# A tile's token numbers go through a second buffer that Pool empties behind its wait for landed additions

## The chip, the cores and the metric

The kernel runs on one core of a Trainium2 chip. The metric is the device time in microseconds (us) from launch to end. The engines are named as in the profile: PE (TensorE, matmuls), DVE (VectorE), ACT (ScalarE), POOL (GpSimd) and SP (SyncE, which here only issues transfers).

## The reference

Four attention layers and a feed-forward layer run over 8 sequences of 256 tokens with 256 features. The last layer is a mixture of 8 experts, each token going to its best two:

```python
def _moe(x, rw, rb, w1, b1, w2, b2):
    xf = x.reshape(T, D)
    router_weights = jax.nn.softmax(xf @ rw + rb, axis=-1)
    topw, topi = jax.lax.top_k(router_weights, K)              # K = 2 of E = 8
    topw = jax.nn.softmax(topw, axis=-1)
    combine = jnp.zeros((T, E), xf.dtype).at[jnp.arange(T)[:, None], topi].add(topw)
    h = jax.nn.gelu(jnp.einsum('td,edf->etf', xf, w1) + b1[:, None, :], approximate=False)
    eo = jnp.einsum('etf,efd->etd', h, w2) + b2[:, None, :]
    out = jnp.einsum('etd,te->td', eo, combine)
...
x = _layernorm(x + _moe(x, router_w, router_b, e_w1, e_b1, e_w2, e_b2), ln3_g, ln3_b)
```

## The kernel before, in words

The first part (attention, feed-forward, router) ends by writing every token's row twice into `slots_x` in DRAM, sorted by expert and cut into tiles of 256 rows. Beside its 256 features a row carries three more words: its token number, its expert and its share. The second part, `moe_part`, works off 23 such tiles, numbered n = 0 to 22, and then normalises the sum in `x_rows` and stores it.

For each tile, `moe_part` reads the expert's weights `w1` and `w2` (1 MB each) from DRAM, splits each weight and each activation in a high and a low half (ACT rounds, `first_high`, `second_high`, `rows_high`; DVE subtracts, `first_low`, `second_low`, `rows_low`, `hidden_low`) and multiplies on PE with three matmuls for each product. The work is laid out as a pipeline: while PE does `up` of tile n, it does `down` of tile n - 1. Each engine has its own instruction order, written out by hand, in a loop over pairs of tiles (`i` is the tile's parity and picks one of two buffers), and semaphores alone tie the engines together. The orders within one step n are:

- PE: `up(n)`, `turn(n + 1)` (transposes), `down(n - 1)`.
- ACT: four quarters, each `first_high(n + 1)`, then GELU and its high half for tile n; `rows_high(n + 1)`; `second_high(n)`.
- DVE: four times `first_low(n + 1)` and `hidden_low(n)`; `rows_low(n + 1)`; `second_low(n)`; then `row_data(n)`; then `add_bias(n - 1)`.
- POOL: `add_rows(n - 1)`.
- SP, each fetch for tile n + 2 behind a wait: rows, `w1`, then (once `second_low(n)` is done) `w2`, then (once `row_data(n)` is done) the three words of the rows (`about`), then `b1`, then (once `add_bias(n - 1)` is done) a bias; then three register loads that pick the next expert, and the next step.

`row_data` (L1416 to L1426) copies the token numbers to `token[i]`, which Pool's indirect transfers read, and works out `share[i]`. `add_bias` (L1433) moves PE's result from PSUM to `result[i]`. `add_rows` (L1237 to L1247) multiplies `result[i]` by `share[i]` (L1241), drains, waits until the additions of the tile before have landed, and issues two indirect transfers (L1247) that add 128 rows each to `x_rows`. Their semaphore is `added[i]`; an addition counts once it has landed. As two tiles can hold the same token, the additions of one tile start only when those of the tile before are in.

Of the kernel before, what the change touches and what calls it, by code (L numbers as in the profile page):

```python
# [10 lines left out]
U32 = mybir.dt.uint32  # L11
# [5 lines left out]
P = 128  # L17
# [14 lines left out]
GT = GROUP // P  # L32
# [114 lines left out]
def build(nc, t, out):  # L147
    with ExitStack() as ctx:
        def sb(name, shape, dt=F32):
            return ctx.enter_context(nc.sbuf_tensor(name, shape, dt))  # L150

        x_rows = nc.dram_tensor("x_rows", [P * ALL_TILES + 2 * GROUP, D], F32).ap()
        slots_x = nc.dram_tensor("slots_x", [X_TILES * GROUP, ROW], F32).ap()
        ident = sb("ident", [P, P])
        minus_half = sb("minus_half", [P, TILES])
        eps = sb("eps", [P, TILES])
        w1, w2 = sb("w1", [P, KC, FF]), sb("w2", [P, FC, D])
        b1_expert = sb("b1_expert", [P, E, FC + 1])
        tile_expert = sb("tile_expert", [P, PLACES], I32)
        tile_source = sb("tile_source", [P, PLACES], I32)  # L160
        shared = (ident, minus_half, eps, w1, w2, b1_expert, tile_expert, tile_source)
        attention_part(nc, t, x_rows, slots_x, *shared)
        moe_part(nc, t, out, x_rows, slots_x, *shared)
# [915 lines left out]
def moe_part(nc, t, out, x_rows, slots_x, ident, minus_half, eps, w1_first, w2_first, b1, tile_expert, tile_source):  # L1079
    with ExitStack() as ctx:  # L1080
        def sb(name, shape, dt=F32):
            return ctx.enter_context(nc.sbuf_tensor(name, shape, dt))

        def two(name, shape, dt=F32):
            return [sb(f"{name}{i}", shape, dt) for i in range(2)]

        def sem(name):
            return ctx.enter_context(nc.semaphore(name))
# [10 lines left out]
        about = two("about", [P, GT, ROW - D])  # L1099
# [1 line left out]
        hidden = sb("e_hidden", [P, FC, GROUP])  # L1101
        hidden_hi, hidden_lo = two("e_hidden_hi", [P, FC, GROUP], F32R), two("e_hidden_lo", [P, FC, GROUP], F32R)
        result = two("result", [P, GT, D])
        token = two("token", [P, GT], U32)
        chosen = two("e_chosen", [P, GT])
        share = two("share", [P, GT])

# [9 lines left out]
        gate = sem("gate")  # L1117
# [17 lines left out]
        b1_loaded = [sem(f"b1_loaded{i}") for i in range(2)]  # L1135
        down_full = sem("down_full")
        row_data_ready = sem("row_data_ready")
        result_ready = sem("result_ready")
        added = [sem(f"added{i}") for i in range(2)]
        z_loaded = [sem(f"z_loaded{b}") for b in range(B)]  # L1140
# [6 lines left out]
        ADDED = 16 * GT  # L1147
# [87 lines left out]
        @block.gpsimd  # L1235
        def _(pool):
            def add_rows(n, i, nth):  # L1237

                pool.wait_ge(result_ready, n + 1)
                pool.sem_inc(gate, 1)  # L1240
                pool.tensor_tensor(result[i][:], result[i][:], share[i][:].unsqueeze(2).to_broadcast([P, GT, D]), ALU.mult)  # L1241
                pool.drain()  # L1242

                pool.wait_ge(added[1 - i], ADDED * nth)
                pool.sem_inc(gate, 1)
                for m in range(GT):
                    pool.indirect_dma_start(x_rows, bass.IndirectOffsetOnAxis(ap=token[i][:, m:m + 1], axis=0), result[i][:, m, :], None, compute_op=ALU.add).then_inc(added[i], 16)  # L1247

            for i in range(2):
                pool.memset(result[i][:], 0.0)  # L1250
                pool.iota(token[i][:], pattern=[[1, GT]], base=P * ALL_TILES + i * GROUP, channel_multiplier=GT)
            pool.drain()
            pool.sem_inc(gate, 1)
            for i in range(2):
                for m in range(GT):
                    pool.indirect_dma_start(x_rows, bass.IndirectOffsetOnAxis(ap=token[i][:, m:m + 1], axis=0), result[i][:, m, :], None).then_inc(added[i], 16)
            with pool.Fori(0, PAIRS) as j:
                for i in (1, 0):
                    n = j * 2 + 2 - i

                    add_rows(n - 1, 1 - i, j + 2 - i)
            add_rows(last_tile, 0, PAIRS + 1)

            def inverse_root(pair):
                both = slice(pair * 2 * TILES, (pair + 1) * 2 * TILES)
                pool.wait_ge(var_ready, pair + 1)
                pool.tensor_tensor(rstd[:, both], var_eps[:, both], minus_half[:, 0:1].to_broadcast([P, 2 * TILES]), ALU.pow).then_inc(rstd_ready, 1)  # L1267

            def gain_of(b):
                pool.wait_ge(normal_ready, b + 1)  # L1270
                pool.tensor_tensor(z[b][:], z[b][:], gain[:].unsqueeze(1).to_broadcast([P, TILES, D]), ALU.mult).then_inc(gained, 1)  # L1271

            pool.wait_ge(norm_loaded, 16 * 2)
            inverse_root(0)
            inverse_root(1)
            gain_of(0)
            inverse_root(2)
            gain_of(1)
            gain_of(2)
            inverse_root(3)  # L1280
            for b in range(3, B):
                if b not in GAIN_BY_DVE:
                    gain_of(b)
# [114 lines left out]
        def _(dve):  # L1398
            def first_low(s, i, q):
                dve.wait_ge(w1_hi_ready, s * QUARTERS + q + 1)  # L1400
                cols = slice(q * 2 * P, (q + 1) * 2 * P)
                dve.tensor_tensor(w1_lo[i][:, :, cols], w1[i][:, :, cols], w1_hi[i][:, :, cols].bitcast(F32), ALU.subtract).then_inc(w1_lo_ready, 1)

            def second_low(s, i, q):
                dve.wait_ge(w2_hi_ready, s * QUARTERS + q + 1)
                dve.tensor_tensor(w2_lo[i][:, 2 * q:2 * q + 2, :], w2[i][:, 2 * q:2 * q + 2, :], w2_hi[i][:, 2 * q:2 * q + 2, :].bitcast(F32), ALU.subtract).then_inc(w2_lo_ready, 1)  # L1406

            def rows_low(n, i):
                dve.wait_ge(rows_hi_ready, n + 1)
                dve.tensor_tensor(rows_lo[i][:].rearrange("p k g -> p (k g)"), turn_bank[i][:], rows_hi[i][:].bitcast(F32).rearrange("p k g -> p (k g)"), ALU.subtract).then_inc(rows_lo_ready, 1)  # L1410

            def hidden_low(n, i, q):
                dve.wait_ge(hidden_hi_ready, n * QUARTERS + q + 1)
                dve.tensor_tensor(hidden_lo[i][:, 2 * q:2 * q + 2, :], hidden[:, 2 * q:2 * q + 2, :], hidden_hi[i][:, 2 * q:2 * q + 2, :].bitcast(F32), ALU.subtract).then_inc(hidden_lo_ready, 1)  # L1414

            def row_data(i, nth, loads):  # L1416

                dve.wait_ge(about_loaded[i], 16 * loads)
                dve.wait_ge(b1_loaded[i], 16 * loads)
                dve.wait_ge(added[i], ADDED * nth)  # L1420
                dve.tensor_copy(token[i][:], about[i][:, :, 0].bitcast(U32))  # L1421
                dve.tensor_scalar(chosen[i][:], about[i][:, :, 1], b1_e[i][:, FC:FC + 1], 1.0, ALU.is_equal, ALU.subtract)
                dve.drain()  # L1423
                dve.tensor_tensor(chosen[i][:], chosen[i][:], about[i][:, :, 2], ALU.add)  # L1424
                dve.drain()
                dve.scalar_tensor_tensor(out=share[i][:], in0=chosen[i][:], scalar=-1.0, in1=chosen[i][:], op0=ALU.mult, op1=ALU.max).then_inc(row_data_ready, 1)  # L1426

            def add_bias(n, i, nth):

                dve.wait_ge(b2_loaded[i], 16 * nth)  # L1430

                dve.wait_ge(down_full, n + 1)
                dve.tensor_tensor(result[i][:], down_bank[i][:].rearrange("p (g d) -> p g d", g=GT), b2_e[i][:].unsqueeze(1).to_broadcast([P, GT, D]), ALU.add).then_inc(result_ready, 1)  # L1433

# [7 lines left out]
                    rows_low(1, 1)  # L1442
            for q in range(QUARTERS):
                second_low(0, 0, q)
            row_data(0, 1, 1)
            with dve.Fori(0, PAIRS) as j:
                for i in (1, 0):
                    n = j * 2 + 2 - i
                    for q in range(QUARTERS):
                        first_low(n + 1, 1 - i, q)  # L1450
                        hidden_low(n, i, q)
                    rows_low(n + 1, 1 - i)
                    for q in range(QUARTERS):
                        second_low(n, i, q)
                    row_data(i, j + 2 - i, j + 2 - i)
                    add_bias(n - 1, 1 - i, j + 1)
            add_bias(last_tile, 0, PAIRS + 1)

            def moments(b):
# [98 lines left out]
```

## Time and profile before

| | |
|---|---|
| median of 3 runs | 1256.54 us (1251.69 to 1257.38) |
| profiled execution: its time, its span | 1253.78 us, 1252.0 us |
| mean granted TensorE clock | 0.950 of full speed |
| busy share of the span: PE, DVE, ACT, POOL | 88%, 66%, 58%, 40% |
| attention part | 0 to 910 us of the span |
| expert tiles, first addition of biases to the last but one | 941.06 to 1207.50 us |
| last additions landed, final norm begins | 1224.58 us |

Time is counted from the start of the span. A step is one round of the expert loop, one tile; 21 steps lie between the two add-bias operations of the table's sixth row, so one takes 12.69 us on average. The busy shares are means over parts with different limits, so only the stretch from 910 us on speaks about the change.

### The profile page before, as it was taken

The page shows a single profiled execution, that of the slowest core. Times are in us where ns is not written, and L with a number is a line of the kernel's source. Part 1 is how long each engine was busy: PE and PEld are TensorE (multiplying, and loading weights), DVE is VectorE, ACT ScalarE, POOL GpSimd, SP SyncE. Part 2 cuts the span into 40 slices and gives each one's busy share as a digit, 9 for nine tenths or more (in the row PEclk, how much of TensorE's full clock was granted, in tenths as well). Part 3 has the DMA queues.
Part 4 walks back from the last instruction along what each step waited for, and adds up shares of the span by engine and source line. Part 5 has one row for each costly group of instructions (what it writes and reads, how often), then busy time and mean ns, then how long its engine had stood idle before and what let it go on. Part 6 is the DMA issues. An engine that isn't in the chain of part 4 may idle for free. (4 is left out here: it accounts for less than half of the span.)

```text
span 1252.0 us, 27029 instructions
## 1 busy us (share of the span) xinstructions
PE 1105.5 (88%) x8981; PEld 910.5 (73%) x8981; DVE 823.3 (66%) x2495; ACT 729.1 (58%) x1537; POOL 501.6 (40%) x709
## 2 busy tenths in 40 slices
PE   8688889999999999998889988977969999999960
PEld 7466667767888878876667756655869899999960
DVE  2667878775555555557776777752457788887846
ACT  4345555665555554545566755645177787887842
POOL 4344555332111223335565455323313334343444
PEclk9789999999999999999999999977889999999985
DMA  7575747564234333435756556504367687867764
GB/s 165 87 117 129 118 71 104 77 127 60 47 45 56 52 52 52 86 53 81 143 88 93 86 88 101 86 27 162 133 231 212 181 232 208 240 206 221 219 189 143
DMA packets 110313, 152.35 MB, mean 122 GB/s; under 512 B 23041, under 2 KB 94977, under 8 KB 103425
## 3 DMA queue, kind: packets, MB, share of 16 engines
q1 hardware_dynamic: 101712, 140.21, 51.2%
q0 software_dynamic: 8352, 10.80, 4.5%
q8 instruction: 56, 0.92, 0.3%
q14 instruction: 49, 0.39, 0.2%
q10 hardware_dynamic: 144, 0.02, 0.0%
HBM read 78.39 MB, written 21.62 MB: 80 GB/s over the span
## 5 line engine op out<-in xcount | busy, mean ns | idle before, releaser
L875 ACT ACTIVATE probs<-s 128x384 f32<-128x384 f32 (+1 forms) x512 | 265.9, 542 | 194.2 <-PE s L683 173.6
L946 DVE TENSOR_REDUCE neg_max<-s 128x2 f32<-128x512 f32 x256 | 169.7, 689 | 94.5 <-PE s L658 84.9
L683 PE MATMUL s<-q_stack,k_stack 98*128 98x256 bf16 (+1 forms) x1024 | 177.6, 263 | 14.4 <-ACT probs L875 13.3
L541 POOL TENSOR_SCALAR_AFFINE_SELECT probs<-probs 128x256 f32<-128x256 f32 x256 | 102.3, 409 | 180.3 <-ACT probs L875 180.3
L943 DVE CUSTOM_DVE_ANT_0 s<-s,mask_qk 128x256 f32<-128x256 f32 x256 | 114.2, 446 | 87.0 <-PE s L655 79.5
L1299 PE MATMUL moe<-rows_hi,e_w_hi 128*128 128x256 f32 x368 | 106.6, 290 | 17.2 <-DVE rows_lo L1410 17.2
L683 PEld LDWEIGHTS s<-q_stack,k_stack 98*128 98x128 bf16 x1024 | 91.3, 99 | 40.2 <-ACT probs L875 24.4
L702 PE MATMUL pv<-probs,v 128*32 128x256 f32 (+1 forms) x2048 | 116.5, 370 | 4.0 <-POOL probs L541 3.9
L658 PE MATMUL s<-k_stack,q_stack 96*128 96x256 bf16 x512 | 98.0, 276 | 13.0 <-DVE neg_max L946 11.3
L1299 PE MATMUL moe<-e_w_hi,e_hidden_hi 128*128 128x256 f32 x368 | 104.7, 284 | 1.2 <-DVE e_w_lo L1406 1.2
L604 PE MATMUL work<-hT,w_qk 128*128 128x256 f32 x384 | 96.1, 395 | 10.2 <-ACTq L797 10.2
L1299 PE MATMUL moe<-rows_lo,e_w_hi 128*128 128x256 f32 x368 | 105.1, 286 | 0.0
L1299 PE MATMUL moe<-rows_hi,e_w_lo 128*128 128x256 f32 x368 | 104.9, 285 | 0.0
L1299 PE MATMUL moe<-e_w_lo,e_hidden_hi 128*128 128x256 f32 x368 | 102.9, 280 | 0.0
L1299 PE MATMUL moe<-e_w_hi,e_hidden_lo 128*128 128x256 f32 x368 | 102.7, 279 | 0.0
L1247 POOL DMA_INDIRECT x_rows<-result,token x46 | 84.1, 1828 | 35.4 <-issue 31.5
L702 PEld LDWEIGHTS pv<-probs,v 128*32 128x32 f32 x2048 | 62.4, 113 | 46.0 <-issue 21.9
L1414 DVE TENSOR_TENSOR e_hidden_lo<-e_hidden,e_hidden_hi 128x512 fp32r<-128x512 f32 x92 | 81.0, 880 | 20.6 <-ACT e_hidden_hi L1374 17.1
L1241 POOL TENSOR_TENSOR result<-result,share 128x512 f32<-128x512 f32 x23 | 30.3, 1316 | 155.9 <-DVE result L1433 155.9
L654 PE MATMUL s<-k_stack,q_stack 96*128 96x256 bf16 x256 | 71.5, 281 | 22.4 <-DVE neg_max L944 17.3
L604 PEld LDWEIGHTS work<-hT,w_qk 128*128 128x128 f32 x384 | 71.7, 196 | 22.7 <-ACTq L797 12.2
L1299 PEld LDWEIGHTS moe<-rows_hi,e_w_hi 128*128 128x128 f32 x368 | 72.3, 197 | 20.0 <-issue 18.1
(194 smaller groups left out, 2696.9 us busy)
## 6 DMA issues: line engine op xcount, KB each, us to landing
w<-in_expert_w SPq DMA_DIRECT2D x26, 1024.0 KB, 5.4
k_stack<-k_part SPq DMA_DIRECT2D x192, 128.0 KB, 4.1
q_stack<-q_part SPq DMA_DIRECT2D x192, 128.0 KB
e_w<-in_expert_w SPq DMA_DIRECT2D x24, 1024.0 KB
rows<-slots_x SPq DMA_DIRECT2D x25, 256.0 KB
slots_x<-filler SPq DMA_DIRECT2D x8, 518.0 KB
cT<-in_context SPq DMA_DIRECT2D x16, 256.0 KB, 4.5
e_b<-in_expert_b SPq DMA_DIRECT2D x24, 128.0 KB
```

Source lines behind the costliest of these rows:

```text
L541: pool.affine_select(out=blocks, in_=blocks, compare_op=ALU.is_ge, fill=0.0, base=0, pattern=[[0, TILES], [1, P]], channel_multiplier=-1). ...
L604: last = pe.matmul(dst[:, half * S:(half + 1) * S], w[:, k, half * P:(half + 1) * P], src[:, k, :], start=(k == 0), stop=(k == KC - 1))
L654: pe.matmul(dst[:, 0:S], q[:, P:S], k, start=True, stop=True)
L658: last = pe.matmul(dst[:, qt * S:(qt + 1) * S], q[:, qt * P:(qt + 1) * P], k, start=True, stop=True)
L683: last = pe.matmul(dst[:, kt * S:kt * S + S - q0], k[:, kt * P:(kt + 1) * P], q[:, q0:S], start=True, stop=True)
L702: last = pe.matmul(pv[32 * j:32 * j + 32, g * S + q0:(g + 1) * S], v[n % 3][:, kt, hd, :], probs[hd][:, kt * S:kt * S + S - q0], start=(kt ...
L875: act.activation(probs[hd][:, 0:width], s2[hd % 2][:, 0:width], ACT.Exp, scale=SCALE).then_inc(probs_ready, 1)
L943: dve.tensor_tensor_reduce(src[:, 0:S], src[:, 0:S], mask_qk[:].rearrange("p b s -> p (b s)"), -1.0, -MASKED, ALU.add, ALU.min, neg_max[:, ...
L946: dve.tensor_reduce(neg_max[:, :, hd], src[:].rearrange("p (t s) -> p t s", t=TILES), AX_X, ALU.max, negate=True).then_inc(s1_free, 1)
L1247: pool.indirect_dma_start(x_rows, bass.IndirectOffsetOnAxis(ap=token[i][:, m:m + 1], axis=0), result[i][:, m, :], None, compute_op=ALU.add ...
L1299: last = pe.matmul(dst, lhs[a], rhs[b], start=first and m == 0, stop=end and m == 2)
L1414: dve.tensor_tensor(hidden_lo[i][:, 2 * q:2 * q + 2, :], hidden[:, 2 * q:2 * q + 2, :], hidden_hi[i][:, 2 * q:2 * q + 2, :].bitcast(F32), ...
```

## The change

DVE now writes the token numbers to a new buffer `token_next[i]`, and Pool copies them to `token[i]` behind its wait for the landed additions of the tile before. A new semaphore, `row_data_taken`, tells DVE that `token_next[i]` (and with it `share[i]`) has been used. The wait for `added[i]` leaves `row_data`, and `add_bias` gets one, on the buffer that it is about to overwrite, which is that of tile n - 3 in step n.

```diff
-        token = two("token", [P, GT], U32)
+        token, token_next = two("token", [P, GT], U32), two("token_next", [P, GT], U32)
...
             def add_rows(n, i, nth):
 
+                pool.wait_ge(row_data_ready, n + 1)
                 pool.wait_ge(result_ready, n + 1)
                 pool.sem_inc(gate, 1)
                 pool.tensor_tensor(result[i][:], result[i][:], share[i][:].unsqueeze(2).to_broadcast([P, GT, D]), ALU.mult)
...
                 pool.wait_ge(added[1 - i], ADDED * nth)
                 pool.sem_inc(gate, 1)
+                pool.tensor_copy(token[i][:], token_next[i][:]).then_inc(row_data_taken, 1)
+                pool.drain()
                 for m in range(GT):
...
             pool.drain()
-            pool.sem_inc(gate, 1)
+            pool.sem_inc(row_data_taken, 1)
...
                 dve.wait_ge(b1_loaded[i], 16 * loads)
+                if nth is not None:
+                    dve.wait_ge(row_data_taken, nth)
+                dve.tensor_copy(token_next[i][:], about[i][:, :, 0].bitcast(U32))
...
             def add_bias(n, i, nth):
 
                 dve.wait_ge(b2_loaded[i], 16 * nth)
                 dve.wait_ge(added[i], ADDED * nth)
-                dve.tensor_copy(token[i][:], about[i][:, :, 0].bitcast(U32))
...
-            row_data(0, 1, 1)
+            row_data(0, None, 1)
...
-                    row_data(i, j + 2 - i, j + 2 - i)
+                    row_data(i, n, j + 2 - i)
                     add_bias(n - 1, 1 - i, j + 1)
```

On DVE, at the end of the loop's first step (odd n, so tile n is in buffers 1), the rows before the change are these; `added1` counts the landed additions of tile n - 2:

```order
L1406 TENSOR_TENSOR e_w2_lo1<-e_w2,e_w2_hi1 128x512 [waits w2_hi_ready] x4
L1418 ISA
L1420 REGISTER_ALU [waits b1_loaded1,about_loaded1]
L1421 COPY token1<-about1 128x2 [waits added1]
L1422 TENSOR_SCALAR e_chosen1<-about1,e_b1_1 128x2
L1424 TENSOR_TENSOR e_chosen1<-e_chosen1,about1 128x2
L1426 SCALAR_TENSOR_TENSOR share1<-e_chosen1 128x2
L1433 TENSOR_TENSOR result0<-moe4,e_b2_0 128x512 [waits down_full,b2_loaded0]
```

And these with the change, where `added0` counts the landed additions of tile n - 3:

```order
L1410 TENSOR_TENSOR e_w2_lo1<-e_w2,e_w2_hi1 128x512 [waits w2_hi_ready] x4
L1422 ISA
L1426 COPY token_next1<-about1 128x2 [waits row_data_taken,b1_loaded1,about_loaded1]
L1427 TENSOR_SCALAR e_chosen1<-about1,e_b1_1 128x2
L1429 TENSOR_TENSOR e_chosen1<-e_chosen1,about1 128x2
L1431 SCALAR_TENSOR_TENSOR share1<-e_chosen1 128x2
L1436 REGISTER_ALU [waits b2_loaded0]
L1438 TENSOR_TENSOR result0<-moe4,e_b2_0 128x512 [waits down_full,added0]
```

The instructions keep their places; the wait for additions has moved from the copy to the last row, and to an older tile.

On Pool, in the loop's second step and the last tile, the rows before are these:

```order
L1241 TENSOR_TENSOR result1<-result1,share1 128x512
L1244 ISA
L1247 DMA x_rows<-result1,token1 2560x256 x2
L1257 REGISTER_ALU
L1257 COMPARE_AND_BRANCH
L1241 TENSOR_TENSOR result0<-result0,share0 128x512
L1247 DMA x_rows<-result0,token0 2560x256 x2
```

And these with the change:

```order
L1243 TENSOR_TENSOR result1<-result1,share1 128x512
L1246 ISA
L1248 COPY token1<-token_next1 128x2
L1251 DMA x_rows<-result1,token1 2560x256 x2
L1261 REGISTER_ALU
L1261 COMPARE_AND_BRANCH
L1243 TENSOR_TENSOR result0<-result0,share0 128x512
L1248 COPY token0<-token_next0 128x2
L1251 DMA x_rows<-result0,token0 2560x256 x2
```

A small copy (and, not printed, a drain) now stands between the wait for the earlier additions and the two transfers. The order on PE, ACT and SP is what it was.

## Rows read from the trace of the kernel before

**Rows 1.** Stretches of the span: PE, PEld, DVE, ACT, POOL busy, clock, DMA

```profile
941.06:1207.50 266.44, 252.29 (x2115) 250.06 (x2115) 211.55 (x379) 213.96 (x441) 105.34 (x63) 0.98 0.75 218
1207.50:1224.58 17.08, 2.35 (x20) 2.15 (x19) 1.39 (x3) 0.00 (x0) 8.41 (x6) 0.64 0.48 106
```

**Rows 2.** Waits from 900 to 1210 us: total us, times, longest us

```profile
DVE token L1421 <- DMA x_rows<-result,token: 37.6, 21, 5.2
ACT e_w_hi L1347 <- DMA e_w<-in_expert_w: 28.2, 11, 5.0
...
ACT e_w_hi L1347 <- DMA w<-in_expert_w: 15.7, 10, 3.0
...
PE moe L1299 <- DVE rows_lo L1410: 17.2, 12, 3.7
```

**Rows 3.** Chain of work that ended last, one step: start us, us, what

```profile
1095.37 0.70 DVE result L1433
1096.22 1.35 POOLq L1242
...
1101.06 5.55 DMA x_rows<-result,token
1107.35 0.70 DVE result L1433
```

**Rows 4.** DVE's timeline, the end of that step and after

```profile
1102.67 0.68 DVE L1410 TENSOR_TENSOR rows_lo<-moe,rows_hi 128x512 fp32r<-128x512 f32 x1
1103.27 2.49 DVE L1406 TENSOR_TENSOR e_w_lo<-w,e_w_hi 128x512 fp32r<-128x512 f32 x4
1106.63 0.17 DVE L1421 COPY token<-about 128x2 uint32<-128x2 uint32 x1 [0.87 <-DMA x_rows<-result,token]
...
1108.56 1.53 DVE L1414 TENSOR_TENSOR e_hidden_lo<-e_hidden,e_hidden_hi 128x512 fp32r<-128x512 f32 x1
```

**Rows 5.** SP's timeline: fetches of w1 (L1162) and w2 (L1165)

```profile
985.58 0.33 SPq L1162 DMA_DIRECT2D e_w<-in_expert_w  x1
...
1088.07 0.33 SPq L1162 DMA_DIRECT2D e_w<-in_expert_w  x1
...
1105.93 0.33 SPq L1165 DMA_DIRECT2D w<-in_expert_w  x1
...
1112.37 0.33 SPq L1162 DMA_DIRECT2D e_w<-in_expert_w  x1
```

**Rows 6.** ACT's timeline: the first rounding of each fetched w1

```profile
994.14 0.63 ACT L1347 ACTIVATE e_w_hi<-e_w 128x512 fp32r<-128x512 f32 x1 [4.99 <-DMA e_w<-in_expert_w]
...
1094.07 0.63 ACT L1347 ACTIVATE e_w_hi<-e_w 128x512 fp32r<-128x512 f32 x1 [2.55 <-DMA e_w<-in_expert_w]
...
1119.41 0.64 ACT L1347 ACTIVATE e_w_hi<-e_w 128x512 fp32r<-128x512 f32 x1 [3.35 <-DMA e_w<-in_expert_w]
```

**Rows 7.** Pool's groups over the whole span: busy, mean ns of one

```profile
L1247 POOL DMA_INDIRECT x_rows<-result,token x46 | 84.1, 1828 | 35.4 <-issue 31.5 <-DMA x_rows<-result,token 3.9
...
L480 POOL TENSOR_TENSOR var_eps_main<-mean_var_main,eps 128x2 f32<-128x2 f32 x24 | 4.7, 197 | 59.9 <-DVEq L905 59.3
...
L1251 POOL IOTA token<- 128x2 uint32 x2 | 0.3, 131 | 0.0
```

**Rows 8.** Tile `token`: transfers' us from issue to landing

```profile
DMA to landing us min/median/max: 3.8/6.4/10.0
```

**Rows 9.** Chain of work that ended last, the tail

```profile
1207.50 0.70 DVE result L1433
...
1218.18 0.74 issue
...
1220.79 3.77 DMA x_rows<-result,token
```

**Rows 10.** Pool's timeline around the change's new copy

```profile
1108.23 1.31 POOL L1241 TENSOR_TENSOR result<-result,share 128x512 f32<-128x512 f32 x1 [5.39 <-DVE result L1433]
1110.64 2.09 POOL L1247 DMA_INDIRECT x_rows<-result,token  x1 [1.10 <-issue]
```

**Rows 11.** A stretch of 2 us behind an idle PE: busy, clock

```profile
1130.00:1132.00 2.00, 2.00 (x14) 2.00 (x13) 1.09 (x2) 0.00 (x0) 0.00 (x0) 0.59 0.77 126
```

More of the change, by code:

```diff
@@ L1137, in moe_part @@
         row_data_ready = sem("row_data_ready")
+        row_data_taken = sem("row_data_taken")
         result_ready = sem("result_ready")
@@ L1419, in row_data @@
                 dve.wait_ge(b1_loaded[i], 16 * loads)
-                dve.wait_ge(added[i], ADDED * nth)
-                dve.tensor_copy(token[i][:], about[i][:, :, 0].bitcast(U32))
+                if nth is not None:
+                    dve.wait_ge(row_data_taken, nth)
+                dve.tensor_copy(token_next[i][:], about[i][:, :, 0].bitcast(U32))
                 dve.tensor_scalar(chosen[i][:], about[i][:, :, 1], b1_e[i][:, FC:FC + 1], 1.0, ALU.is_equal, ALU.subtract)
@@ L1430, in add_bias @@
                 dve.wait_ge(b2_loaded[i], 16 * nth)
+                dve.wait_ge(added[i], ADDED * nth)
                 dve.wait_ge(down_full, n + 1)
```

## The prediction

> **What bounds the kernel now.** I began with the page's split of the span: the change touches only the expert part, so I cut the rest off with the view by stretches. From the first add-bias to the last but one (L1433 at 941.06 and 1207.50 us), 21 steps take 266.44 us, 12.69 us each, and PE is busy for 252.29 of them [rows 1]. So PE leaves 14.2 us, and everything the change can win lies near that figure.
>
> Then the view of waits. DVE stands still 37.6 us, 21 times, before its copy of the token numbers, for additions to land: 1.79 us a step. ACT stands still 28.2 + 15.7 = 43.9 us, 21 times, for `w1`. PE stands still 17.2 us, 12 times, for `rows_lo` of DVE [rows 2].
>
> The chain of waits shows how the first closes on itself: add-bias at 1095.37, Pool's product, the second transfer at 1101.06, its landing after 5.55, and the next add-bias at 1107.35, 11.98 us later [rows 3]. In the 21 steps the last link is always a landing. Yet a chain names only the last releaser; I need to know what is late next.
>
> DVE's and SP's timelines give that. `second_low` ends at 1103.27 + 2.49 = 1105.76, SP issues `w2` at 1105.93, DVE idles 0.87 until the landing, and SP reaches the next `w1` only at 1112.37, since that stands on SP's queue behind `row_data`, behind `add_bias` and behind three register loads [rows 4, 5]. That `w1` is what ACT starts on at 1119.41, and ACT's start at 1094.07 is what led to it [rows 6]. This is a second loop, over two steps: ACT start 1094.07, fetch 1112.37 (18.30 later, 0.87 of it the stall), landing 7.04 later: 25.34 us. The first loop and this one share the stall.
>
> **The change part by part.**
>
> 1. It removes the wait at the token copy: 1.79 us a step [rows 2]. Queued behind it on DVE were the share, add-bias and the next step's `first_low`; waiting on those were Pool (idle anyway until add-bias), SP (`about`, a bias, and behind them `w1`) and ACT through `w1`.
>
> 2. It adds a wait at add-bias for tile n - 3. The landing of tile n - 2 now comes about when DVE gets there, so that of n - 3 came one step, some 12 us, earlier: cost 0. It also adds a wait in `row_data` for Pool's copy for tile n - 2. Pool makes that within 2.4 us of the product's start (its transfer begins at 1110.64 where the product begins at 1108.23 [rows 10]), most of a step ahead of need: cost 0. That cover is gone only if a landing is a whole step late; the longest one took 10.0 against a median of 6.4 [rows 8], 3.6 late. Pool's new wait for `row_data_ready` is always met, since DVE does it before add-bias.
>
> 3. It adds a copy of 128x2 words and a drain on Pool, behind the wait for landing and ahead of the transfers. The trace has no such copy. The nearest rows are the two-input operation of the same size, 0.197 us, and the iota of that size, 0.131 us [rows 7]. For the drain, the gap from the product's end to the transfer is 1.10 us with a drain in it [rows 10], and from a landing to the transfer 0.74 without one [rows 9]: 0.36 at most as a difference, 0 at least. Copy and drain together: 0.13 to 0.56, taken as 0.45, as I see nothing that hides the drain. In a step this is covered: from landing to landing the additions need 0.74 + 1.83 + 0.30 (between the transfers) + 6.4 = 9.3 us [rows 7 to 9], 9.7 with the copy, against 12. Only at the end is it bare: tiles 21 and 22 follow each other without cover, from 1207.50 to the last landing at 1224.56 [rows 9]. Cost 2 x 0.45 = +0.9 us, once.
>
> 4. A price on DVE. While Pool's product ran (1108.23 for 1.31), a `hidden_low` took 1.53 us where others take 0.68, 0.85 more [rows 4, 10]. The new copy lands among the same DVE operations, so it can hold one for up to its own 0.2 us. It would count half in the two-step loop: at most 0.1 x 21 = 2.1 us. I take 0, because DVE idles before several of these for ACT; 2.1 goes into the range.
>
> The Trainium skill speaks against the change here: "SBUF — State Buffer", section "SBUF: two separate sides", says that VectorE with two SBUF inputs and a GpSimd operation that reads SBUF exclude each other for a whole instruction. The 1.53 us row agrees. By that rule each copy costs at some point up to a DVE operation's 0.68 us of waiting on Pool, and the sum would be 0.7 a tile worse in the tail, 1.4 in all, and otherwise the same.
>
> 5. What is late next. The fetch loop without the stall: 2 x 12.69 - 1.79 = 23.6 us, 11.8 a step. Against it, the fetch itself may get slower. From SP's issue to ACT's start took 6.25 us on average over 20 fetches, 5.35 at least and 8.56 at most (985.58 to 994.14; others here are 1088.07 to 1094.07 and 1112.37 to 1119.41 [rows 5, 6]). I sorted these by DVE's stall just before. After the eight stalls up to 1.1 us the fetch took 6.59; after the twelve longer ones 6.03. The stall spaces out `w2` (issued ahead of it) from the additions and `w1` (issued behind it); without it they overlap more. So I add 0.5 us to a fetch, near the difference of 0.56: 24.1 for two steps, 12.04 for one. PE itself needs 252.29 / 21 = 12.01, with stretches at 0.59 of the clock, that is partly at 1.2 GHz, behind its idle times [rows 1, 11]; its steps at full clock took 11.7. PE is thus just under the fetch loop.
>
> **Sum.** 21 x (12.69 - 12.04) = 13.7 us won, 0.9 lost in the tail: 12.8. The profiled execution took 1253.8 us, so 1241.0. The three runs have their median at 1256.5 and reach from 1251.7 to 1257.4; I set the kernel before at 1255, between the two, and forecast **1242**.
>
> **The rivals.**
>
> - *PE is next, not the fetch* (17%). The fetch keeps to 6.0 or less, and with PE never idle its clock holds: 11.7 a step. 21 x 0.99 = 20.8, less 0.9: 19.9, so 1235. For it: fetches of 5.4 us are frequent. Against it: the sorted fetches.
>
> - *The stall moves to the fetch* (18%). With `w2`, additions and `w1` on the queues at once, a fetch gets slower by 1.2 to 1.8 us, most or all of the stall that left the two-step loop, and the step stays at 12.4 to 12.7: 1250 to 1256. For it: two of the fetches took over 7.4 us, one 8.56, all beside additions, and DMA is 75% busy already [rows 1]. Against it: transfers now only move by 1.8 us in a step of 12. That a wait survives under another name (the new semaphore, or add-bias on an old tile) would give the same time; item 2 speaks against it.
>
> - *Slower: the additions become the loop* (8%). They are one behind the other by Pool's wait, and now each has a copy and drain within. It decides once a landing takes over 12.69 - 3.3 = 9.4 us on average; then Pool falls behind, add-bias waits for the older landing and everything with it. At 9.9 the step is 13.2, 21 x 0.5 + 0.9 = 11 us more: 1266. One landing of 10.0 shows that it happens, the median of 6.4 [rows 8] that it isn't the rule.
>
> - The forecast: 57%, from 1238 to 1250 by itself (fetch slower by 0.2 to 1.1 us, copy holding DVE or not).
>
> **How the numbers follow.** A measurement of this kernel can tell about 0.5%, 6.3 us, from no change, so "same" is 1250 to 1263. Faster: the forecast, the PE rival and part of the second, 0.57 + 0.17 + 0.02, less some for spread, 0.75. Same 0.17, slower 0.08. The range for 8 in 10 takes in the PE rival's 1235 and most of the second rival's: 1234 to 1255.
>
> **What would show it.** In the changed kernel DVE's copy to `token_next` has no wait for additions (none of the 37.6 us); PE's wait for `rows_lo` falls from 17.2 us to some 5 and its stretches at the low clock mostly go; ACT still waits for `w1`, some 1.2 us a step instead of 2.1; SP's fetch to ACT's start takes 6.5 to 6.9 on average; the step is 12.0 us; Pool's copy takes 0.13 to 0.2; the tail from the last but one add-bias to the last landing is 18 us rather than 17. I am wrong if fetches take over 8 us (second rival), if Pool waits for landings ahead of its copy in most steps (third), or if a wait for `row_data_taken` or `added` shows on DVE.

## The result and the profile after

The changed kernel took 1232.73 us (median of 4 runs, 1230.59 to 1234.83) against 1254.12 (4 runs, 1247.55 to 1257.38): a ratio of 0.9836, with a 95% interval of 0.9805 to 0.9867, so 1.6% faster. I had forecast 1242 and given 1234 to 1255. In a later batch of runs the same kernel took 1233.06 us, but the kernel before took 1244.35 there: 0.9909, 0.9888 to 0.9930. The new time stayed and the old one moved; what is known of that stands at the end of the account of the prediction.

The view by stretches, cut at the same events as [rows 1] (the first row is added, the time before the first add-bias):

```profile
908.76:940.82 32.06, 24.67 (x169) 24.10 (x170) 20.71 (x40) 25.21 (x49) 5.53 (x8) 0.79 0.66 222
940.82:1186.06 245.24, 245.24 (x2105) 245.24 (x2104) 209.27 (x378) 215.15 (x440) 117.00 (x84) 1.00 0.79 237
1186.06:1204.30 18.24, 3.96 (x34) 3.75 (x32) 1.39 (x3) 0.00 (x0) 8.79 (x8) 0.71 0.49 108
```

The 21 steps fell from 266.44 to 245.24 us, 11.68 each, and PE is busy for all of it at the full clock. PE's busy time itself fell from 252.29 to 245.24. So of the 21.2 us, 14.2 were idle time and 7.0 were busy time, which went as the granted clock rose from 0.98 to 1.00. The tail, from the last but one add-bias to the last landing, grew from 17.08 to 18.24. The first add-bias came 0.24 us earlier than before, and the stretch behind the tail differs by 0.1.

The waits from 900 to 1190 us, the ones that answer to [rows 2]:

```profile
ACT e_hidden L1375 <- PE moe L1303: 11.5, 17, 1.2
...
ACT e_w_hi L1351 <- DMA e_w<-in_expert_w: 8.5, 10, 1.9
...
ACT e_w_hi L1351 <- DMA w<-in_expert_w: 3.7, 4, 1.5
...
PE moe L1303 <- DVE rows_lo L1414: 2.3, 1, 2.3
```

DVE no longer waits for a landing at all, nor for `row_data_taken`. ACT waits 12.2 us for `w1` instead of 43.9, and now waits for PE. PE waits for `rows_lo` once, before the first add-bias. The chain of waits, where [rows 3] had landings, is now PE alone, step after step:

```profile
1108.39 0.44 PE moe L1297 x4
1108.82 11.31 PE moe L1303 x96
1120.13 0.44 PE moe L1297 x4
1120.57 11.11 PE moe L1303 x96
```

Pool's timeline, in a step and in the tail; it answers to [rows 10]:

```profile
1105.35 1.32 POOL L1243 TENSOR_TENSOR result<-result,share 128x512 f32<-128x512 f32 x1 [4.50 <-issue]
1107.15 0.71 POOL L1248 COPY token<-token_next 128x2 uint32<-128x2 uint32 x1 [0.48 <-issue]
1108.66 1.81 POOL L1251 DMA_INDIRECT x_rows<-result,token  x1 [0.80 <-issue]
...
1188.44 0.19 POOL L1248 COPY token<-token_next 128x2 uint32<-128x2 uint32 x1 [0.47 <-issue]
```

The copy takes 0.71 us in a step and 0.19 in the tail, where DVE stands still. From the product's end to the first transfer took 1.10 us before and now takes 1108.66 - 1106.67 = 1.99.

### The profile page after: what moved, and what is told of

Same layout as the page of the kernel before. It is cut to its first block and busy times, and to the rows that moved or that the text cites. A ratio compares the mean times of both kernels' runs of the same rounds, so it can differ in the third digit from the quotient of the medians.

```text
span 1231.6 us, 27064 instructions
## 1 busy us (share of the span) xinstructions
PE 1099.5 (89%) x8981; PEld 907.1 (74%) x8981; DVE 821.4 (67%) x2495; ACT 729.9 (59%) x1537; POOL 513.8 (42%) x732
## 5 line engine op out<-in xcount | busy, mean ns | idle before, releaser
L604 PE MATMUL work<-hT,w_qk 128*128 128x256 f32 x384 | 94.9, 391 | 10.8 <-ACTq L797 10.8
L1418 DVE TENSOR_TENSOR e_hidden_lo<-e_hidden,e_hidden_hi 128x512 fp32r<-128x512 f32 x92 | 76.6, 833 | 39.5 <-ACT e_hidden_hi L1378 30.5
L1251 POOL DMA_INDIRECT x_rows<-result,token x46 | 80.5, 1750 | 25.2 <-issue 25.2
L944 DVE CUSTOM_DVE_ANT_0 s<-s,mask_qk 128x128 f32<-128x128 f32 x256 | 84.9, 332 | 0.0
L1375 ACT ACTIVATE e_hidden<-moe,e_b 128x256 f32<-128x256 f32 x184 | 75.9, 463 | 11.6 <-PE moe L1303 11.5
```

Source lines behind the costliest of these rows:

```text
L604: last = pe.matmul(dst[:, half * S:(half + 1) * S], w[:, k, half * P:(half + 1) * P], src[:, k, :], start=(k == 0), stop=(k == KC - 1))
L944: dve.tensor_tensor_reduce(src[:, S:S + P], src[:, S:S + P], mask_qk[:, 1, :], -1.0, -MASKED, ALU.add, ALU.min, neg_max[:, 0, hd:hd + 1]). ...
```

## The experiments

Each batch has its own runs of the kernel before; ratios are against those. "Step" is the time from the first add-bias to the last but one in the profile, divided by 21.

**The wait put back (e1_wait_back).**

```diff
                     dve.wait_ge(row_data_taken, nth)
+                    dve.wait_ge(added[i], ADDED * loads)
```

> The changed kernel with DVE's wait for the landed additions of tile n - 2 put back in front of the copy in row_data; the second buffer, Pool's copy and its drain stay. Theory: the whole gain is that wait. From the product's end to the first transfer Pool took 1.12 us before and takes 1.99 with the copy and drain, and here these 0.87 us lie in the landing loop again: the step is 12.69 + 0.87 = 13.5 us, and the time is about 18 us above before, near 1272. Rival: something else in the change wins (the later write of token, the wait at add-bias): the time stays near 1233. Second rival: the landing loop has slack besides its stall, and the time is that of before, 1254.

1247.1 us against 1245.05, ratio 1.0022 (1.0003 to 1.0041). The gain is gone, so the wait is what the change wins by. But of the 18 us more only 2 came. That is the second rival's time, yet not for its reason, slack in the landing loop: the profile has DVE's wait for a landing again, in all 21 steps:

```profile
DVE token_next L1427 <- DMA x_rows<-result,token: 40.2, 21, 3.9
```

So the landings must have made up for the 0.87 us by which Pool starts its additions later. From the second transfer's issue to DVE's copy they took 5.32 us on average over the 21 steps (5.31, from 1007.78 to 1013.09, and 4.78, from 1020.13 to 1024.91, in two steps in a row), against 6.42 in the profile of the kernel before. The step is (1198.93 - 939.23) / 21 = 12.37 us. Neither figure compares cleanly with that profile: it is from another batch, in which the kernel before took 9 us more, and it was not profiled beside this run. So how much of the shorter landing is due to the copy's delay stays open.

**Add-bias ahead of row_data, nothing else (e2_swap).**

```diff
-                    row_data(i, j + 2 - i, j + 2 - i)
                     add_bias(n - 1, 1 - i, j + 1)
+                    row_data(i, j + 2 - i, j + 2 - i)
```

> The kernel before with one edit: in DVE's loop add_bias(n - 1) stands ahead of row_data(n), with its wait; no second buffer and no copy. Theory: what costs is that the landing of tile n - 2 holds up add-bias of tile n - 1, and so the next additions. With the order turned, a landing 11.3 us after its add-bias meets a wait 11.68 + 0.7 us after it, so no stall, PE sets the step at 11.68, and the tail keeps its 17.1 us (18.2 with the copy): about 1232. Rival: any wait for the landing on DVE costs, wherever it stands, since first_low stands behind it: then 1240 to 1254.

1249.36 us against 1245.05, ratio 1.0028 (1.0003 to 1.0052): no gain, and my theory for it fell. The time is the rival's, but not for its reason: DVE's wait for landings did go; the profile has none. In its place the chain of waits runs through the fetches of `w1`:

```profile
1004.34 0.38 SPq L1174
...
1005.58 0.44 SPq L1168
...
1008.75 0.39 SPq L1171
1009.34 6.53 DMA e_w<-in_expert_w
```

`row_data` now ends after add-bias. SP issues `about` 2.25 us after `second_low` ended (999.60 + 2.49 = 1002.09 to 1004.34), where it was 0.94 us without the stall (1105.76 to 1107.57, less 0.87), and `w1` follows behind. That is 1.3 us more, in every step. Of it, 0.8 us are one small operation of `row_data`, which now runs while Pool's product does and took 0.96 us instead of 0.16:

```profile
1002.97 0.96 DVE L1424 TENSOR_TENSOR e_chosen<-e_chosen,about 128x2 f32<-128x2 f32 x1
```

The fetch loop, 1.3 us longer over two steps, took back what the landing loop gave up: with this run's fetches of 6.54 us on average (18 of them) and the 17.35 us of the rest of the loop (23.6 - 6.25, as in the prediction) it is (17.35 + 1.3 + 6.54) / 2 = 12.6, and the step is (1205.25 - 938.44) / 21 = 12.71. e8_swap_ahead tests this.

**Copy and drain twice (e3_double_copy).**

```diff
+                pool.tensor_copy(token[i][:], token_next[i][:])
+                pool.drain()
                 pool.tensor_copy(token[i][:], token_next[i][:]).then_inc(row_data_taken, 1)
                 pool.drain()
```

> The changed kernel with Pool's copy and drain made twice. Theory: in a step they are covered, as PE sets it at 11.68 us and from landing to landing the additions need about 10 us; only the tail pays, twice about 0.4 us to 1 us: 1233 to 1235. Rival: the copy (0.72 us in a step, 0.19 in the tail) holds up DVE, which takes it from PE: 21 x 0.4 to 0.7, so 1242 to 1248.

1231.67 us, ratio 0.9903 (0.9883 to 0.9924); the step is (1183.50 - 938.38) / 21 = 11.67. The copies, with medians of 0.71 and 0.51 us, are covered in every step. The rival is out.

**Less work for PE (e4_less_pe).**

```diff
-                             [w[i][:, f, :] for w in (w2_hi, w2_lo)], f == 0, f == FC - 1)
+                             [w[i][:, f, :] for w in (w2_hi, w2_lo)], f == 0, f == FC - 1, ((0, 0), (1, 0)))
```

> The changed kernel with one of the three products of down (high half of the hidden values by low half of w2) left out, 16 of 96 matmuls of a step; all waits stay. It uncovers what comes next after PE, which then needs some 9.8 us a step. If the fetch loop stands as predicted (6.75 us for a fetch, 12.04 us a step) nothing is won: the step stays at 11.7 or more, 1233 or above. If a fetch takes 5.4 us, as in the changed kernel's trace, the loop is at (17.4 + 5.4) / 2 = 11.4 and the time near 1227. If neither binds, ACT's 10.5 us does, and the time is near 1210.

(`pair_products` takes the list of products as an argument for this, which is not printed.) 1230.79 us, ratio 0.9888 (0.9862 to 0.9914); the step is (1185.50 - 938.76) / 21 = 11.75, no shorter than with all of PE's work. The fetch loop is the next bound, level with PE: PE now waits for `rows_lo` again, 32.4 us in 19 times, and e7_less_pe_ahead takes this loop away. The 17 fetches that ACT waited for took 5.99 us on average; with the 17.35 us of the rest of the loop that gives (17.35 + 5.99) / 2 = 11.67. Fetches here were 5.0 to 7.6 us, so its price was between the two that I had offered.

**Fetching ahead on SP (e5 to e8).** In all four, SP issues the next step's rows and `w1` ahead of this step's `w2`, `about` and biases:

```diff
-                    step(n, i, e, at)
+                if not last:
+                    ahead(n + 1, 1 - i, expert(n + 3), source(n + 3))
+                behind(n, i, e, at)
                 sp.wait_ge(result_ready, n)
                 fetch_bias(next_e, 1 - i)
```

`ahead` holds the waits and fetches of rows and `w1`, `behind` the rest of `step`, unchanged.

On the kernel before (e5_ahead):

> The kernel before with SP's order alone changed: the rows and w1 for the next step are fetched as soon as their buffers are free, ahead of this step's w2, about and biases, so w1 no longer stands behind row_data, add-bias and the register loads. That takes the fetch loop away and leaves the landing loop. Theory: the landing loop by itself holds the step above PE's 11.68 us; DVE goes on waiting for landings, over 20 us in all, and at most half of the gain comes: 1237 to 1245. Rival: the fetch loop was the one that really bound, and DVE's wait follows from it; then the wait falls under 10 us and the time is that of the changed kernel, about 1231.

1275.85 us against 1252.84, ratio 1.0190 (1.0161 to 1.0219): slower, which neither theory had. The fetch loop is indeed gone, and ACT waits for PE. The landing loop holds the step at (1232.42 - 940.22) / 21 = 13.91 us:

```profile
DVE token L1443 <- DMA x_rows<-result,token: 77.9, 21, 7.4
ACT e_hidden L1393 <- PE moe L1321: 65.8, 25, 7.1
```

Its landings took longer in the chain: 7.85 us on average over 20, against 6.40. So the landing loop holds the step without the fetch loop, and its own length changed when SP's fetches went out at other times. Which of these fetches lengthens a landing, the runs don't separate.

On the changed kernel (e6_after_ahead):

> The changed kernel with the same fetching ahead on SP. Theory: PE sets each step at 11.68 us already, so a fetch loop taken away gives nothing: within 0.3% of the changed kernel, 1229 to 1234. Rival: the changed kernel is on both bounds at once and some steps are lost to late fetches: up to 4 us less.

1231.55 us, ratio 0.9846 (0.9812 to 0.9880), as the theory had it; the step is (1184.86 - 939.72) / 21 = 11.67. Pool waits for landings 14 times here (22.1 us in all), which does not reach PE.

On the kernel with less work for PE (e7_less_pe_ahead):

> e4_less_pe (one product of down left out, 80 of 96 matmuls of a step kept) with the fetching ahead. There the step stayed at 11.75 us though PE needs 9.8. Theory: the fetch loop held it; with it gone the step falls to ACT's 10.5 to 10.8 us, 21 x 1.1 = 23 us less, about 1208. Rival: the landings or DVE hold it, and it stays at 1225 or above.

1219.07 us, ratio 0.9735 (0.9705 to 0.9764); the step fell from 11.75 to (1175.03 - 945.60) / 21 = 10.93. That shows the fetch loop in e4_less_pe. I had said 1208. The step is 0.1 to 0.4 us above the 10.5 to 10.8 that I had; the rest of the miss is not accounted for. (The profiled execution took 1224.02, the longest of the four; in it the expert part began 5 us later than in the changed kernel's, its first matmuls at 917.22 against 912.42.) In the steps, Pool now waits for landings (69.9 us in 20 steps), so the additions are near their own limit.

On the swapped kernel (e8_swap_ahead):

> e2_swap (the kernel before with add-bias ahead of row_data) with the fetching ahead. In e2_swap DVE's wait for landings was gone, and yet the step was 12.7 us, with the fetches of w1 as the chain of waits. Theory: there the swap made row_data end, and so SP's later fetches, 2 us later; that lengthened the two-step fetch loop and ate the gain. With the fetches ahead PE sets the step at 11.68: about 1230, at or 1 us under the changed kernel, as there is no copy in the tail. Rival: the swap costs in another way, and the time stays above 1240.

1229.26 us, ratio 0.9814 (0.9784 to 0.9844); the step is (1187.58 - 942.47) / 21 = 11.67. It confirms what ate the swap's gain: with the fetches out of the way, two reordered lists and no second buffer reach PE's bound.

**Where the copy stands (e9_copy_early), and the changed kernel beside it (e10_after_again).**

```diff
                 pool.wait_ge(row_data_ready, n + 1)
+                pool.wait_ge(added[i], ADDED * own)
+                pool.sem_inc(gate, 1)
+                pool.tensor_copy(token[i][:], token_next[i][:])
                 pool.wait_ge(result_ready, n + 1)
...
                 pool.wait_ge(added[1 - i], ADDED * nth)
                 pool.sem_inc(gate, 1)
-                pool.tensor_copy(token[i][:], token_next[i][:]).then_inc(row_data_taken, 1)
-                pool.drain()
```

> The changed kernel with Pool's copy made ahead of its wait for the result, where Pool idles, and without the second drain; row_data_taken is counted up by the product. The additions then start 0.9 us earlier in a step and 0.9 us nearer to the fetch of w1. Theory: PE sets the step at 11.68 and Pool's copy and drain cost only in the tail, so the tail falls from 18.2 to 17 us and the time by 1 us. Rival: the copy's delay helped: it let SP's fetch of w1 (5.4 us in the kernels with the copy there, 6.2 to 6.5 in those without) go out ahead of the additions; then fetches go back to 6.2 us, the fetch loop rises to about 11.8 to 12 us a step, PE stands idle for rows_lo again, and the time rises by 3 to 7 us.

> The changed kernel itself, for a comparison on the same chip: 1230 to 1234.

1233.95 us, ratio 0.9917 (0.9894 to 0.9941), against 1233.06 and 0.9909 for the changed kernel. The times don't differ, neither as the theory had it nor as the rival had. The profile bears the rival's mechanism out, at a lower price: the step is (1188.20 - 940.27) / 21 = 11.81 against (1187.33 - 942.05) / 21 = 11.68, so 2.7 us in 21 steps, and PE is idle for 1.8 us of them. The theory's shorter tail is not shown: 17.74 us (1188.20 to 1205.94) against 17.77 in the changed kernel beside it (1187.33 to 1205.10). That the 2.7 us don't show in the times is within their scatter; in the two profiled executions the steps of e9_copy_early happened to begin 1.8 us earlier. One fetch of `w1` and what goes out beside it, on Pool, SP and ACT of e9_copy_early:

```profile
1051.21 2.10 POOL L1252 DMA_INDIRECT x_rows<-result,token  x1 [1.10 <-issue]
...
1052.92 0.33 SPq L1163 DMA_DIRECT2D e_w<-in_expert_w  x1
...
1058.66 0.63 ACT L1352 ACTIVATE e_w_hi<-e_w 128x512 fp32r<-128x512 f32 x1 [1.88 <-DMA e_w<-in_expert_w]
```

The first addition is issued 1.71 us ahead of `w1`. In e1_wait_back, which has copy and drain in between, it is 0.85 ahead:

```profile
1005.65 1.82 POOL L1251 DMA_INDIRECT x_rows<-result,token  x1 [0.79 <-issue]
...
1006.50 0.33 SPq L1163 DMA_DIRECT2D e_w<-in_expert_w  x1
...
1011.71 0.63 ACT L1351 ACTIVATE e_w_hi<-e_w 128x512 fp32r<-128x512 f32 x1 [1.75 <-DMA e_w<-in_expert_w]
```

From SP's issue to ACT's start, over the fetches that ACT waited for, from the last one ahead of the first add-bias on:

| kernel | DVE's stall | copy and drain ahead of the additions | fetch of w1, us (count) | step, us |
|---|---|---|---|---|
| before | yes | no | 6.24 (21) | 12.69 |
| e1_wait_back | yes | yes | 5.46 (21) | 12.37 |
| e2_swap | no | no | 6.46 (19) | 12.71 |
| e9_copy_early | no | no | 6.23 (18) | 11.81 |
| changed | no | yes | 5.56 (14) | 11.68 |
| changed, again | no | yes | 5.58 (11) | 11.68 |
| e3_double_copy | no | twice | 5.48 (13) | 11.67 |
| e4_less_pe | no | yes | 5.99 (17) | 11.75 |

DVE's stall makes no difference that can be seen (6.24 against 6.23, 5.46 against 5.56). With copy and drain ahead of the additions a fetch took some 0.7 us less; the one comparison within a batch, with little else changed, is e9_copy_early against the changed kernel again, 6.23 and 5.58. Against a firm 0.7 speak e4_less_pe, which has copy and drain too and whose fetches took 5.99, and that a row knows only the fetches that ACT waited for, in one execution: 14 and 11 of some 22 in the changed kernel.

How the copy shortens a fetch isn't shown. That `w1` goes out nearer to the first addition is not enough as a reason: in the changed kernel the seven fetches that had it 1.26 to 1.47 us ahead took 4.85 to 5.41 us, and the six that had it 0.43 to 0.82 ahead took 5.37 to 6.84.

**Both improvements (e11_early_ahead, e12_swap_ahead_again).** e11 is e9 with the fetching ahead.

> e9_copy_early with SP's fetching ahead as in e6_after_ahead. Both theories: fetches of w1 are no longer late, PE sets 11.68 us, and the tail is the short one: 1 us under e6_after_ahead, 1229 to 1232.

> e8_swap_ahead again beside the changed kernel on one chip, in five rounds: 0 to 3 us under the changed kernel.

1228.98 us, ratio 0.9885 (0.9865 to 0.9905), and 1231.21 us, 0.9892 (0.9867 to 0.9916), beside 0.9909 (0.9888 to 0.9930) for the changed kernel. Both may be 0.2% better than it; the intervals overlap, so that isn't shown. The tail of e11_early_ahead, 17.83 us (1184.95 to 1202.78), is no shorter either.

## Why the prediction was wrong

The direction was right, and the first of my rivals came true: PE is next, not the fetch, 1235 at 17%. By its own steps:

1. *The wait removed.* Right. e1_wait_back shows that the gain is this wait: put back, it takes the whole gain with it. That the 1.79 us would not all be won, as a second loop shares them, was right too.

2. *The waits added at no cost.* Right; neither shows in the profile.

3. *Pool's copy and drain.* I took 0.45 us, and the copy at 0.13 to 0.2. In the tail the copy took 0.19, and the gap from the product's end to the transfer grew from 1.10 to 1.44 us; the tail grew by 1.16 where I had 0.9. Of that, 0.34 and 0.36 are copy and drain ahead of the last two tiles' transfers; the rest is a landing between them that took 6.3 us where it had taken 5.8. In a step copy and drain took 0.89, covered. The 0.71 us are a small copy among DVE's operations. The Trainium skill, "SBUF — State Buffer", section "SBUF: two separate sides", says that a GpSimd operation waits out a VectorE one with two SBUF inputs; 0.71 against 0.19 with DVE at rest agrees. I had worked out 1.4 us in the tail from that rule; but there DVE is at rest, and the waiting lay in the steps, where it is covered.

4. *DVE held up by the copy at 0.* Right for the time: with two copies the step stayed at 11.67.

5. *What is late next.* This step failed: "I add 0.5 us to a fetch, near the difference of 0.56". A fetch took 5.56 us after the change, not 6.75. I had sorted 20 fetches by the stall before them and read a cause into a difference of 0.56 between groups of 8 and 12, whose members lie between 5.35 and 8.56. The table above shows no effect of the stall. It shows fetches that were some 0.7 us shorter behind what I had counted only as a cost, the copy and drain; why is open. With the measured fetch the loop is (17.35 + 5.56) / 2 = 11.46 us, under PE. e4_less_pe, where PE is out of the way, puts it higher, at 11.75, level with PE. Without the copy's delay it is (17.35 + 6.23) / 2 = 11.79, and e9_copy_early's step is 11.81. By each of these the loop lies within 0.25 us of PE's 11.68, and none has it at 12.04. What set the step instead was PE, as the first rival had it, at 11.68. I had 12.04, 0.36 us too much in each of 21 steps: 7.6 of the 9.3 us between 1242 and 1232.7.

The same step set PE's need at 12.01, "just under the fetch loop", though I had named the 11.7 at full clock. The clock loss went with the idle time: in the steps the granted clock rose from 0.98 to 1.00, and PE's busy time fell by 7.0 us. I had given that to the rival only.

*The sum's base.* I set before at 1255 in place of the profile's 1253.8, 1.2 us of the rest. From the profile's own time the right terms give 1253.8 - 21.2 + 1.2 = 1233.8, and the profiled execution took 1233.35.

What stays open: why the kernel before took 1244 to 1254 us in different batches (1245.05, 1252.84 and 1244.35 in the three of the experiments, each on another chip), where the changed one took 1233 in both that it was in. Its steps hang on landings and the changed kernel's on PE, and landings vary; but I have a profile of it from one batch only, so this is argued and not shown.

## What to carry to other kernels

When a stall is on two loops, work out each loop without it, and give the engine that is busiest its time at full clock; the slowest of these is the new step. Don't price contention by sorting twenty transfers by what came before: change what goes out when, and look. An order of instructions that seems neutral can give back a gain (e2_swap), and work that looks like a pure cost can be followed by shorter transfers (the copy and drain). So try the fetching order together with the wait: reordering DVE (e2_swap) or SP (e5_ahead) alone was no faster than before, and both together (e8_swap_ahead) reached the bound.

## What the runs showed of the hardware

A 1 MB fetch beside indirect additions took 6.2 us on average in the kernel before and in e9_copy_early, where the first addition went out 1.3 to 2.0 us ahead of it, and 5.5 us in e1_wait_back, where it went out 0.5 to 0.9 ahead; but in the changed kernel fetches with 1.3 to 1.5 us took 4.9 to 5.4, so the lead alone doesn't set it. An indirect addition of 128 rows landed 3.5 to 3.9 us after its issue when it was the last one, and in 5.5 to 10 us in the steps of the kernel before. A copy of 128x2 words on Pool took 0.19 us with DVE at rest and 0.71 with DVE busy. An operation of 128x2 on DVE took 0.16 us by itself and 0.96 while Pool's product ran (e2_swap).
